# GpSimd takes over the source one-hots of the last block in two edge loops

## What is computed

```python
def _L0_gnn_ref(x, edge_index, W, att_src, att_dst, bias):
    ...
    h = (x @ W.T).reshape(N, H, C)                      # 4 heads of 64
    e = leaky_relu(a_s[src] + a_d[dst], 0.2)            # plus one loop edge per node
    p = exp(e - segment_max(e, dst)[dst])
    alpha = p / (segment_sum(p, dst)[dst] + 1e-16)
    out = segment_sum(alpha[:, :, None] * h[src], dst)
    return elu(out.reshape(N, H * C) + bias) + x

x = x + _L0_gnn_ref(_layernorm(x), ...)      # first edge loop
x = x + _L0_ffn_ref(...)                     # mixture of experts
x = x + _L1_gnn_ref(_layernorm(x), ...)      # two attention layers: second edge loop, then a dense one
x = x + _L1_ffn_ref(...)                     # a recurrence
x = x + _L2_gnn_ref(...) ; x = x + _L2_ffn_ref(...)
x = x + _L3_gnn_ref(...) ; x = x + _L3_ffn_ref(...)
```

## Time and profile before

| | us |
|---|---|
| median of 3 runs | 4454.93 (4453.63 to 4455.15) |
| the profiled execution | 4457.94 |
| its span | 4456.2 |
| PE busy in it | 3571.4 (80%) |
| DVE busy | 2742.4 (62%) |
| ACT busy | 1649.5 (37%) |
| POOL busy | 1262.1 (28%) |
| POOL, gathers of L814 | 837.3, 850 of them |

### The profile page before, as it was taken

One profiled execution on the slowest core, in us unless ns is written; L12 is line 12 of the kernel. 1 busy time (PEld: TensorE's weight loads), 2 busy tenths in 40 slices (PEclk: granted clock), 3 DMA queues, 4 the chain that ended last, 5 costly groups with the idle time before them and its releaser, 6 DMA issues. The chain is left out here.

```text
span 4456.2 us, 67369 instructions
## 1 busy us (share of the span) xinstructions
PE 3571.4 (80%) x23854; PEld 3134.3 (70%) x23854; DVE 2742.4 (62%) x6930; ACT 1649.5 (37%) x4318; POOL 1262.1 (28%) x1266
## 2 busy tenths in 40 slices
PE   4777774844777777998999999799998699959696
PEld 3566653643656566774888888689998599949596
DVE  6898986554888848964777777742234433353444
ACT  1444451212444444552666666521111122320131
POOL 6777741636777710000000000000000122200163
PEclk8788885976888888999999999899998799979798
DMA  5455542244555563500000000143444311153324
GB/s 158 133 159 143 159 116 96 90 105 122 144 158 143 158 166 97 141 1 15 1 1 1 1 1 1 28 119 111 121 119 154 107 37 38 34 134 107 133 71 132
DMA packets 196553, 418.23 MB, mean 94 GB/s; under 512 B 54821, under 2 KB 127659, under 8 KB 195840
## 3 DMA queue, kind: packets, MB, share of 16 engines
q1 hardware_dynamic: 135296, 250.07, 19.8%
q0 software_dynamic: 60928, 164.04, 13.2%
HBM read 329.61 MB, written 84.35 MB: 93 GB/s over the span
## 5 line engine op out<-in xcount | busy, mean ns | idle before, releaser
L814 POOL DMA_INDIRECT sb<-features,sb x850 | 837.3, 985 | 262.2 <-issue 258.6
L1937 PE MATMUL ps<-sb 128*128 128x125 f32 x5400 | 688.5, 283 | 73.9 <-DVE sb L1996 73.2
L1937 PEld LDWEIGHTS ps<-sb 128*128 128x128 f32 x5400 | 636.4, 191 | 126.0 <-DVE sb L1996 115.3
L2223 PE MATMUL ps<-sb 125*125 125x256 f16 x5000 | 571.3, 275 | 15.8 <-DVE sb L2323 15.8
L2223 PEld LDWEIGHTS ps<-sb 125*125 125x125 f16 x5000 | 558.9, 138 | 21.0 <-issue 16.1
L136 POOL IOTA sb<- 128x56 f32 (+9 forms) x30 | 5.5, 219 | 1684.2 <-POOLq L1654 1608.5
L1963 ACT ACTIVATE sb<-ps 128x125 f32<-128x125 f32 x1350 | 360.6, 276 | 255.0 <-PE ps L1937 255.0
L2928 ACT ACTIVATE sb<-ps,sb 128x128 f32<-128x128 f32 x784 | 221.1, 376 | 546.1 <-PE ps L2856 546.1
L1110 PE MATMUL ps<-sb 128*125 128x260 f32 x1700 | 385.2, 385 | 6.9 <-PEq L1108 6.4
L2856 PE MATMUL ps<-sb 128*128 128x128 f32 x3136 | 381.7, 277 | 2.0 <-DVE sb L2897 1.8
L1110 PEld LDWEIGHTS ps<-sb 128*125 128x125 f32 x1700 | 317.4, 188 | 88.3 <-issue 37.1
(11 more groups left out here) (321 smaller groups left out, 5278.5 us busy)
## 6 DMA issues: line engine op xcount, KB each, us to landing
sb<-adj SPq DMA_DIRECT2D x125, 683.6 KB
neg<-sb SPq DMA_DIRECT2D x25, 683.6 KB
adj<-sb SPq DMA_DIRECT2D x25, 683.6 KB
sb<-neg SPq DMA_DIRECT2D x25, 683.6 KB
sb<-rows_y SPq DMA_DIRECT2D x30, 560.0 KB
sb<-in_L_ffn_W SPq DMA_DIRECT2D x16, 1024.0 KB, 12.7
sb<-features,sb POOLq DMA_INDIRECT x850
sb<-adj SPq DMA_DIRECT2D x125, 79.3 KB
```

The costliest lines, as they stand in the source:

```text
L814: e.indirect_dma_start(hgs[i % 4][:, w, :], None, k.HR, indirect(ids[i % 3][:, w:w + 1])).then_inc(*hg_in[i % 4].by(16))
L1937: return e.matmul(k.PS[:, b, 0:NC], V[:, y, row, :], self.old_h(n)[:, y, :], start=False, stop=y == 1, skip_group_check=True)
L2223: m = e.matmul(self.k.PS[0:P, v % 2, 0:D], self.ads[v % self.RING][:, j * P:j * P + P], part[:, j, :], start=j == 0 and x == 0, stop=j == ...
```

## The change

The function `vector_hots` is renamed `make_hots` and does what it did. VectorE calls it as before up to step i = 24 and no longer in the last steps. What falls away there, GpSimd does behind its last gather: in the first loop FIRST and LAST of block 24, in the second LAST of block 23. GpSimd first waits for the block's edge records (`eg_in`), and in the second loop also until the eight products of FIRST are through, since the token doesn't tell one-hots apart.

```diff
-    def vector_hots(self, e, t, eg, ws):
+    def make_hots(self, e, t, eg, ws):
         for w in ws:
             e.wait_ge(*self.used.at(W * (t // 2) + max(w - 3, 0)))
             e.tensor_scalar(self.hots[w % 4][:, 0:FOLD], self.ioF[:, :], eg[:, w, 1:2], eg[:, w, 2:3],
...
                         e.indirect_dma_start(hgs[i % 4][:, w, :], None, k.HR,
                                              indirect(ids[i % 3][:, w:w + 1])).then_inc(*hg_in[i % 4].by(16))
+                b = adj.last
+                e.wait_ge(*eg_in[b % 6].at(16 * (b // 6 + 1)))
+                if b + 1 == T:
+                    adj.make_hots(e, b, egs[b % 6], adj.FIRST)
+                else:
+                    e.wait_ge(*adj.used.at(W * (b // 2) + 8))
+                adj.make_hots(e, b, egs[b % 6], adj.LAST)
...
-                    if adj.has(i - 1):
-                        adj.vector_hots(e, i - 1, egs[(i - 1) % 6], adj.FIRST)
-                    if adj.has(i - 2):
-                        adj.vector_hots(e, i - 2, egs[(i - 2) % 6], adj.LAST)
+                    if adj.has(i - 1) and i < T:
+                        adj.make_hots(e, i - 1, egs[(i - 1) % 6], adj.FIRST)
+                    if adj.has(i - 2) and i < T:
+                        adj.make_hots(e, i - 2, egs[(i - 2) % 6], adj.LAST)
```

## The result

The changed kernel takes 4496.4 us (median of 4 runs, 4493.0 to 4500.6) against 4454.3 us (4 runs, 4452.7 to 4455.2): the ratio is 1.0088, with a 95% interval of 1.0077 to 1.0100, so +34 to +45 us. The forecast was +2 us. The profiled execution took 4500.6 us, with a span of 4498.8.

The account below looks back on a forecast made before the run. GpSimd's gathers bound each edge loop, then VectorE, TensorE and ScalarE its end. Loop shifts -1.8 + 1.8, plus 1 us ports and 1 us clock, gave +2 us: 4457.94 + 2 - 3.0 = 4456.9 us, range 4449.3 to 4467.9.

Parts of the forecast that it names:

- What bounds the kernel, and when GpSimd is free: Edge loops: GpSimd paces up to the last gather, then VectorE, TensorE, ScalarE; GpSimd free from 628.2 and 1575.1 us.
- The price p: Time of one 782-column one-hot on GpSimd: taken as 1.2 us, with 0.78 and 1.67 as ends.
- 18p - 22: Both loops' summed shift in us for a GpSimd one-hot costing p, used at high p; 0 forecast at 1.2.
- Rival 1: GpSimd's two-operation one-hot is slow, compare and multiply in two passes: 2.4 us each, +21 us, 4476 us; chance 0.20.
- First and second loop: Ends of the edge loops, GpSimd only four one-hots ahead: -1.8 us in the first, +1.8 in the second, sum 0.
- (b) Clock: TensorE at half speed after sparse GpSimd-paced products, slowing an add_up: 1 us for both loops, bounds 0 and 2.
- 9p - 12.6: First loop's end: shift of add_up(24) for a GpSimd one-hot costing p; -1.8 us at 1.2.
- 9p - 9.4: Second loop's end: shift once p exceeds 1.3 us and GpSimd misses the first four one-hots; +5.6 at 1.67.
- 4p - 3.3: First loop, FIRST(24): its last product ends this much later for a one-hot costing p; 1.5 us at 1.2.
- (a) Ports: Port contention between VectorE's small operations and GpSimd's one-hots behind the last gathers: 1 us, bounds 0 and 3.
- stretched gathers: First loop: GpSimd gathers beside VectorE's integer shifts take 1.23 and 1.32 us instead of 0.95, so both hold each other up.
- Rival 2: VectorE's relief at the loops' ends counts in full: -12.5 us, 4442.4 us; chance 0.03, shared with any other gain.

Follow-up runs that it names:

- half-width kernel: Changed kernel, but GpSimd's one-hots write only 391 of 782 columns, last blocks' counts wrong; 4473.7 us, ratio 1.0040.
- only first loop: Changed kernel, but GpSimd makes only the first loop's 17 one-hots, second loop as before the change; 4478.2 us against 4454.6, ratio 1.0053.
- only second loop: Changed kernel, but GpSimd makes only the second loop's 9 one-hots, LAST of block 23; 4474.9 us, ratio 1.0043.
- one operation: Changed kernel, but GpSimd's one-hots do the compare alone, without the scale; single run 4478.9 us against 4459.3 before the change.

## Why the prediction was wrong

**What bounds the kernel, and when GpSimd is free:** right. The last gathers start at 627.7 and 1589.7 us in the changed kernel, the first four one-hots run from 631 us.

**The price p: the step that failed.** 1.2 us, with 0.78 and 1.67 as ends; measured 2.98. The two loops' sum above p = 1.3 is 18p - 22: at 2.98 that is +31.6 us, where 0 was forecast. The ends were chosen by how many tensors a row reads and writes, "it reads two tensors where this reads one", and the number of arithmetic operations was left out of them. It is what moves the price of this very instruction, 2.2 and 3.0 us for one and two; the copy takes 0.84. The upper row, the TENSOR_TENSOR at 2.14 ns a column, has two inputs and one operation and was taken for a bound; the new form takes 3.3 ns a column. AFFINE_SELECT, from which the middle was taken, was a line through one width of 128 columns and a fixed part borrowed from other operations: 1.2 to 1.5 ns a column. It neither showed a slope of its own nor the two operations. Rival 1 named the mechanism (two operations in passes), with 2.4 us for p and +21 us; it was given 0.20 and should have had more, as no row of the trace held a `tensor_scalar` with a second operation. Its own 2.4 us still gives only half of the measured loss.

**First and second loop:** the form of the sums was right. Four of a portion are free, each further one costs p; both portions of the first loop and the second loop come out as separate and additive terms. At p = 2.98 they give +14.2 and +17.4 us; the tails show +18.3 and +20.2. The rest is mostly the next point. A small slip stands beside it: VectorE's one-hot was put at 0.48 us, its length, where six in 2.69 us are 0.45 each, so 11.7 and not 12.5 us left VectorE; the sum does not use it.

**(b) Clock:** right in kind, mis-sized: 1 us was taken, with 2 as the upper bound for both loops. The windows of TensorE in the changed kernel, from its start of FIRST(24) on (us, length, busy of PE, PEclk, DMA share, GB/s), and last the same spot before:

```profile
648.00:652.00 4.00, 2.75 (x8) 0.50 0.09 29
652.00:655.00 3.00, 0.88 (x2) 0.50 0.00 0
655.00:662.30 7.30, 2.46 (x7) 0.50 0.11 32
...
651.00:652.00 1.00, 1.00 (x6) 1.00 0.00 0
```

The windows behind it, with PEld, DVE, ACT and POOL between PE and the clock:

```profile
662.30:663.90 1.60, 1.60 (x4) 0.67 (x3) 0.00 (x0) 0.00 (x0) 1.60 (x1) 0.50 0.94 305
663.90:667.90 4.00, 4.00 (x14) 3.22 (x13) 3.50 (x11) 0.00 (x0) 4.00 (x3) 0.68 0.05 16
667.90:672.80 4.90, 4.90 (x27) 4.16 (x25) 0.97 (x4) 0.00 (x0) 4.90 (x2) 1.00 0.00 0
```

TensorE stands at 1.2 GHz when FIRST(24) begins, before the change too (0.50 from 644.0 to 647.2 us). Before, eight products one behind the other bring it back: 1.00 from 651 us. Paced products leave it at 0.50, and what follows starts there: pick takes 1.81 us in place of 0.97, in each loop; add_up 8.91, 9.04 and 8.78 in place of 7.69, and 10.61 in place of 9.66. That is 0.84 + 1.22 + 1.35 = 3.4 us in the first loop and 0.84 + 1.09 + 0.95 = 2.9 in the second. The other kernels can be checked with their own matmuls, which differ: the two add_ups behind the first loop's products in the half-width kernel are

```profile
657.34 8.56 PE L1117 MATMUL ps<-sb 128*125 128x260 f32 x34
...
681.31 10.21 PE L1117 MATMUL ps<-sb 128*125 128x260 f32 x34
```

"Pace" is 9p - 12.6 or 9p - 9.4; "clock" is what pick and the two add_ups take more than before:

| kernel, loop | pace | clock | sum | tail |
|---|---|---|---|---|
| changed, first | 14.2 | 3.4 | 17.6 | 18.3 |
| changed, second | 17.4 | 2.9 | 20.3 | 20.2 |
| only first loop | 14.2 | 4.5 | 18.7 | 20.6 |
| only second loop | 17.3 | 1.0 | 18.3 | 18.2 |
| one operation, first | 7.6 | 4.3 | 11.9 | 13.4 |
| one operation, second | 10.8 | 2.3 | 13.1 | 12.7 |
| half width, first | 2.5 | 4.2 | 6.7 | 6.8 |
| half width, second | 5.7 | 2.6 | 8.3 | 8.1 |

The second loop comes out within 0.4 us. The first is 0.1 to 1.9 us short. Its steps agree less well than its sum: from the start of FIRST(24) to that of pick it is 14.4 us in the changed kernel (647.90 to 662.28) against 4.2 before, 10.2 us more where 4p - 3.3 gives 8.6; and of the clock's 3.4 us not all lengthens the path, since pick runs in part in a gap that TensorE had ahead of add_up(23) (0.36 us).

**(a) Ports:** 0 to 3 us was taken; alone it is 7.9 us on the tails where VectorE has no slack. In the changed kernel the visible part is on GpSimd's side, as the prediction's stretched gathers had it: the eight one-hots from 648.89 us take 24.42 us, where the first four, in 11.89, have 23.8 for eight. These 0.6 us fall into the four of FIRST(24), where VectorE's shifts run beside them (from 653.5 us), and TensorE waits for them. Single operations of VectorE are held too, but it is GpSimd that TensorE waits for. The rule of the Trainium skill (SBUF — State Buffer, Who interferes with whom), that the engine that issues first has the shared ports for its whole instruction and the other is blocked, agrees with the direction, not with the length: operations of VectorE were held for up to 1.2 us beside instructions of 3 us. In the second loop the logits end at 1595.9 us, not with the fourth one-hot at 1602.6, as the prediction had worked out from that rule.

**Rival 2, the whole relief of VectorE:** excluded as argued. Even a MEMSET at 0.75 us brings 6.6 us in the first loop's tail, not the 17 x 0.45 = 7.7 that leave VectorE there, and nothing in the second.

## What to carry to other kernels

An engine that is idle is not free capacity until its price for that very form is measured: put the instruction, into a spare tile, where the engine idles, and look at more than one width. When work is moved to a slower engine behind a short ring of buffers, only as many pieces as the ring holds are hidden; every further one costs the slower engine's full price on the path, and here TensorE, waiting between them, also came out at the lower clock. Bounds for an operation that the trace doesn't hold must cover each thing in which it differs from the nearest row (here inputs, width and number of operations), not only one.

## What the runs showed of the hardware

GpSimd's `tensor_scalar` at 128x782: 2.9 to 3.3 us with two operations and 2.2 with one, whatever the types and the kind of scalar; the f16 to bf16 copy 0.84 us, a bf16 MEMSET 0.75. With two operations the widths 200, 391 and 782 take 1.06, 1.68 and 2.98 us. VectorE's same two-operation form takes 0.48 us, and 0.45 one behind the other. Work on GpSimd that nobody waits for cost the kernel 7 us (3.6 to 11.6); single operations of VectorE of several kinds grew beside it, from 0.17 to 0.97, from 0.29 to 1.44 and from 0.42 to 1.09 us, more than half of them begun just as one of GpSimd began, while the same forms at other moments did not grow. Pick and the add_ups behind products 1.7 to 3.4 us apart took 1.8 us in place of 0.97 and 8.6 to 10.2 in place of 7.69, at a granted clock of 0.50 at their start.
